# Adding the last tile's results by matmuls with a 0/1 matrix, and three moves in the order of work

## The chip, the cores and the metric

The kernel runs on one core of one Trainium2 chip. The metric is the device time of one execution in microseconds. Before the change it is 1116.69 us, the median of three runs (1115.52, 1116.69 and 1117.11).

## The reference

The input x has 4 batches of 512 rows of 256 numbers. The first half is a gated cross attention, the second a gated mixture of experts:

```python
x = x + tanh(g_xattn) * attention(layernorm(x), ctx)       # 16 heads of 64, ctx: 4 x 1024 rows,
                                                           # keys rotated by cos and sin, scores clipped to +-11
logits = xf @ wr + br                                      # xf = layernorm(x), 4 experts
gates = softmax(top_k(logits, 2))
h = gelu(xf @ w1[e] + b1[e]); y = h @ w2[e] + b2[e]        # hidden width 1024
c[e] = gelu(b1[e]) @ w2[e] + b2[e]
x = x + tanh(g_ffn) * sum_k gates_k * (y_sel - c_sel + sum_e c[e])
```

Each row of x is therefore computed by its two best experts and gets the two weighted results added.

## The kernel before, in words

Every product of two matrices of importance is done in three matmuls on numbers split into a high part (rounded to fp32r) and a low part (the remainder): high by high, high by low, low by high. The function `three` issues them. ScalarE usually makes the high part, VectorE or GpSimd the low part. There is one instruction stream for each engine, written out by hand, and semaphores join them; the order inside a stream is the order of the code.

**Start.** `before()` normalises the first context batch, turns its tiles on TensorE, and makes keys and values of the first unit. The weights for keys and values come in four parts (one for each unit of four heads) and are split by `wkv_round` (ScalarE) and `wkv_low` (VectorE, L1179). Their raw numbers share memory with the probabilities. TensorE waits once for the first part and once, at the end of `before()`, for all four.

**Attention.** Four batches, four units in each, eight steps in each unit. A step makes two score tiles (L1848), ScalarE takes their exponential (L957), VectorE clamps (L1199) and sums them (L1211, L1214), TensorE multiplies the step before by the values (L1864). In the same step TensorE makes the next unit's keys and values of one tile (`kv_make`), ScalarE brings the keys to `k_raw` (L902), GpSimd and VectorE rotate them (`rotate`, L733 and L737 on GpSimd, L1187 on VectorE), TensorE turns them (`k_turn`, L1834) and they are split (L895, L1151).

**Routing.** In the last batch, steps 17 to 26, GpSimd scatters the rows of the first three batches into slots in DRAM, sorted by expert, by indirect DMAs (`scatter`, L773): two in each of the steps 17 to 23, and in the steps 24 to 26 four, three and three. They wait for records of VectorE (`rec_out`). In the steps up to 23 a rotation follows them, in step 19 also the low part of the next query weights (`wq_low`, L722), in step 24 the low part of the output weights (`wo_low`, L726), for which SyncE's next load of output weights waits, and behind that its loads of expert weights.

**Experts.** 19 jobs (`JOBS`) of 256 slots, each with eight hidden parts m of 128 columns. For n = 8 job + m TensorE issues `outputs(n)` and then `hidden(n + 3)`. Between them ScalarE takes the Gelu (L1070), ScalarE (m in `ACT_HIGHS` = 1, 2, 3, 5, 7; L1075) or VectorE (others; L1677) makes the high part and VectorE the low part (L1680). GpSimd makes low parts of the next job's first weights (L803) and scatters the results of a finished job to the rows' places in `tokens_y` (`scatter_y`, L791), after VectorE has weighted them by the gates (`copy_slots`, L1694). The last batch's 512 rows are routed later: `rank_gates` in job 3 (m = 5), the exponential on ScalarE in job 4 (m = 6, L1105), `late_spill`, `late_bases`, `late_places` on VectorE in job 4 (m = 5, 6, 7), `last_gates`, `late_slots` with `records`, `late_owners` in job 5 (m = 5, 6, 7).

**End.** Six loads of 512 KB bring the results of the first three batches (`load_tokens`), VectorE adds them to x in the jobs 17 and 18 (`add_tokens`, L1705). After the last job its results are weighted, scattered, and then the last batch's results are loaded in eight parts of 128 KB by SyncE (L660) and ScalarE's queue (L1113), added by VectorE in eight instructions (`add_last`, L1713), and stored.

## Time and profile before

| | |
|---|---|
| median of three runs | 1116.69 us |
| profiled execution | 1115.35 us |
| its span | 1113.6 us |
| busy: PE, DVE, ACT, POOL | 1069.4, 942.0, 656.2, 530.9 us |
| granted TensorE clock, mean | 0.992 |

PE is TensorE's matmuls, DVE is VectorE, ACT is ScalarE, POOL is GpSimd, SPq and ACTq are the instructions by which SyncE and ScalarE issue DMAs. Times in the trace count from the span's start. A busy PE is one with a matmul in it; the ends of matmuls are modelled, and successive ones overlap. In square brackets stands how long the engine was idle before an instruction and what it then waited for. The granted clock is a share of 2.4 GHz, so 0.5 is the level of 1.2 GHz.

### The profile page before, as it was taken

The page shows a single profiled execution, that of the slowest core. Times are in us where ns is not written, and L with a number is a line of the kernel's source. Part 1 is how long each engine was busy: PE and PEld are TensorE (multiplying, and loading weights), DVE is VectorE, ACT ScalarE, POOL GpSimd, SP SyncE. Part 2 cuts the span into 40 slices and gives each one's busy share as a digit, 9 for nine tenths or more (in the row PEclk, how much of TensorE's full clock was granted, in tenths as well). Part 3 has the DMA queues.
Part 4 walks back from the last instruction along what each step waited for, and adds up shares of the span by engine and source line. Part 5 has one row for each costly group of instructions (what it writes and reads, how often), then busy time and mean ns, then how long its engine had stood idle before and what let it go on. Part 6 is the DMA issues. An engine that isn't in the chain of part 4 may idle for free.

```text
span 1113.6 us, 22458 instructions
## 1 busy us (share of the span) xinstructions
PE 1069.4 (96%) x7949; PEld 712.0 (64%) x7949; DVE 942.0 (85%) x1767; ACT 656.2 (59%) x1267; POOL 530.9 (48%) x550
## 2 busy tenths in 40 slices
PE   5899999999999999999999999998999998999994
PEld 3556555655555555656555655655556998899994
DVE  7798999898989989898999898888878756776675
ACT  5555556664645765554656655544667666567662
POOL 7433475332437634342565353325751654755561
PEclk9999999999999999999999999999999999999998
DMA  7000010000000000001010000601164333555335
GB/s 207 17 11 11 20 39 11 20 11 11 11 19 25 25 11 11 18 4 30 5 39 15 11 11 11 195 11 35 54 217 156 117 118 116 181 205 172 115 118 177
DMA packets 59190, 72.05 MB, mean 65 GB/s; under 512 B 11580, under 2 KB 52168, under 8 KB 59081
## 3 DMA queue, kind: packets, MB, share of 16 engines
q1 hardware_dynamic: 54840, 61.30, 17.7%
q0 software_dynamic: 3360, 8.53, 2.0%
q8 instruction: 66, 1.08, 0.4%
q10 hardware_dynamic: 880, 0.79, 0.2%
q14 instruction: 44, 0.35, 0.1%
HBM read 54.84 MB, written 16.54 MB: 64 GB/s over the span
## 4 chain that ended last, share of the span: by engine, by line
PE 80%; DVE 12%; issue 3%; ACT 2%; POOL 1%; DMA 1%; SPq 0%; DVEq 0%; ACTq 0%; POOLq 0%
PE pv L1864 17%; PE sc L1848 15%; PE kv L1793 6%; PE kv L1795 5%; PE kv L1794 5%; PE sc L1793 5%; PE sc L1794 4%; PE sc L1795 4%; PE tr L1834 3%; PE mi L1793 3%; PE mi L1794 2%; PE mi L1795 2%; DVE acc L1214 2%; PE mi L1874 2%; DVE prob L1199 1%
## 5 line engine op out<-in xcount | busy, mean ns | idle before, releaser
L957 ACT ACTIVATE prob<-sc 128x1024 f32<-128x1024 f32 x256 | 249.2, 1029 | 198.7 <-PE sc L1848 196.2
L733 POOL TENSOR_TENSOR rot_s<-k_raw,sinb 128x256 f32<-128x256 f32 x128 | 109.8, 858 | 380.8 <-ACT k_raw L902 380.5
L1864 PE MATMUL pv<-prob,val 128*32 128x512 f32 x1984 | 237.8, 597 | 0.7 <-DVE recip L1233 0.7
L1199 DVE TENSOR_SCALAR prob<-prob 128x1024 f32<-128x1024 f32 x256 | 179.7, 714 | 44.4 <-ACT prob L957 42.2
L1848 PE MATMUL sc<-q_hid,w2all 64*128 64x512 f32 x1536 | 212.5, 408 | 1.2 <-DVE w2all L1179 1.2
L1848 PEld LDWEIGHTS sc<-q_hid,w2all 64*128 64x128 f32 x1536 | 134.7, 184 | 101.2 <-issue 54.2
L1214 DVE TENSOR_TENSOR acc<-acc,prob 128x1024 f32<-128x1024 f32 x120 | 178.0, 1504 | 0.0
L737 POOL TENSOR_TENSOR rot_c<-rot_c,rot_s 128x256 f32<-128x256 f32 x128 | 111.0, 867 | 34.1 <-DVE rot_c L1187 19.1
L1864 PEld LDWEIGHTS pv<-prob,val 128*32 128x32 f32 x1984 | 54.8, 109 | 106.0 <-issue 85.6
L1793 PE MATMUL kv<-w2all,acts 128*128 128x512 f32 x248 | 109.7, 442 | 2.2 <-DVE acts L1145 1.3
L1795 PE MATMUL kv<-w2all,acts 128*128 128x512 f32 x248 | 98.7, 398 | 0.0
L1794 PE MATMUL kv<-w2all,acts 128*128 128x512 f32 x248 | 98.0, 395 | 0.0
L1793 PE MATMUL sc<-w2all,q_hid 128*128 x304 | 89.9, 296 | 7.5 <-DVE q_hid L1680 6.0
L1794 PE MATMUL sc<-w2all,q_hid 128*128 x304 | 86.1, 283 | 0.0
L1795 PE MATMUL sc<-w2all,q_hid 128*128 x304 | 85.8, 282 | 0.0
L1211 DVE TENSOR_TENSOR acc<-prob 128x1024 f32<-128x1024 f32 x60 | 84.5, 1447 | 0.0
L902 ACT ACTIVATE k_raw<-kv 128x256 f32<-128x256 f32 x124 | 48.6, 392 | 53.5 <-PE kv L1795 51.6
L1187 DVE TENSOR_TENSOR rot_c<-kv,cosb 128x256 f32<-128x256 f32 x124 | 52.3, 422 | 31.6 <-ACT val L903 25.8
L1680 DVE SCALAR_TENSOR_TENSOR q_hid<-sc,rot_c,q_hid 128x256 fp32r<-128x256 f32 x78 | 37.5, 482 | 35.7 <-ACT q_hid L1075 30.3
L1793 PEld LDWEIGHTS sc<-w2all,q_hid 128*128 128x128 f32 x304 | 58.0, 191 | 11.5 <-issue 11.2
L1070 ACT ACTIVATE sc<-sc,c_aff 128x256 f32<-128x256 f32 x78 | 34.9, 448 | 51.4 <-PE sc L1795 51.4
L803 POOL TENSOR_TENSOR acts<-prob,acts 128x512 fp32r<-128x512 f32 x34 | 44.8, 1319 | 40.5 <-ACT acts L990 39.4
(326 smaller groups left out, 2400.0 us busy)
## 6 DMA issues: line engine op xcount, KB each, us to landing
prob<-in_L_ffn_w SPq DMA_DIRECT2D x17, 1024.0 KB
slots_x<-lat_r SPq DMA_DIRECT2D x1, 5016.0 KB, 18.9
rows<-slots_x SPq DMA_DIRECT2D x19, 264.0 KB, 5.2
rows<-in_ctx SPq DMA_DIRECT2D x32, 128.0 KB, 2.2
w_raw<-in_L_xattn_Wq SPq DMA_DIRECT2D x16, 256.0 KB, 2.7
w_raw<-in_L_xattn_Wo SPq DMA_DIRECT2D x64, 64.0 KB
acc<-in_L_ffn_w SPq DMA_DIRECT2D x16, 256.0 KB, 5.0
acc<-in_L_ffn_w SPq DMA_DIRECT2D x5, 512.0 KB
```

What stands on the lines that cost most here:

```text
L733: g.tensor_tensor(rot_s[:].rearrange("p (h a c) -> p h a c", h=4, a=2), kh[:, :, ::-1, :], sinb[:, t].unsqueeze(1).to_broadcast([P, 4, 2, ...
L737: g.tensor_tensor(k_rot[:], rot_c[:], rot_s[:], ALU.add).then_inc(rot, 1)
L957: a.activation(prob[:, s % 2, i, :], sc[i][:], ACT.Exp, scale=DH ** -0.5).then_inc(exp_done[i], 1)
L1187: v.tensor_tensor(rot_c[:].rearrange("p (h c) -> p h c", h=8), kv_bank(b, u, t)[:, 0:UW].rearrange("p (h c) -> p h c", h=8), cosb[:, t].un ...
L1199: v.tensor_scalar(prob[:, s % 2, i, :], prob[:, s % 2, i, :], EXP_LOW, EXP_HIGH, ALU.max, ALU.min).then_inc(clamped[i], 1)
L1211: v.tensor_tensor(acc[:, i, :], prob[:, 0, i, :], prob[:, 1, i, :], ALU.add).then_inc(summed[i], 1)
L1214: v.tensor_tensor(acc[:, i, :], acc[:, i, :], prob[:, s % 2, i, :], ALU.add).then_inc(summed[i], 1)
L1793: mm(dst, lhs(0), rhs(0), start=start, stop=False, **kw)
L1794: mm(dst, lhs(0), rhs(1), start=False, stop=False, **kw)
L1795: return mm(dst, lhs(1), rhs(0), start=False, stop=stop, **kw)
L1848: last = mm(sc[i][:, h * N:(h + 1) * N], kst[rows_h, u % 2, j, lk, t * P:(t + 1) * P], q_sp[rows_h, p % 2, lq, :], start=lk + lq == 0, sto ...
L1864: last = mm(out_bank(b, p)[g * 32:(g + 1) * 32, :], val[:, u % 2, 2 * c + i, at:at + 32], prob[:, s % 2, i, h * N:(h + 1) * N], start=c == ...
```

## The change

1. **The last tile.** The results of the last job (`LAST`) aren't scattered any more. All their rows belong to the last batch. ScalarE and VectorE weight them by the gates and split them in high and low, VectorE has built a matrix that is 1 where a slot's row is (`one_hot`, from `last_places` and an iota of GpSimd, in job 18 at m = 3), and 16 matmuls with it as the stationary operand add up the rows in two banks, from which `add_last` adds them to x. The other tiles' results for the last batch are loaded in two DMAs of 512 KB, once job 17 is scattered, into the memory of the raw weights, and added by `add_rows`. Places of `tokens_y` that nobody writes any more must be zero, so SyncE clears those of the last batch in the last batch's step 8 (1 MB). In job 18 ScalarE makes all high parts, `copy_slots` of job 17 comes at m = 1 instead of 2, and `add_tokens` at m = 0, 2, 4, 6 instead of 1, 3, 5, 7. The second half of job 18's output goes to another bank.
2. **Late gates.** The exponential of the last batch's logits is computed by GpSimd as a power of e, in its stream ahead of the scatter of job 2's results. `last_gates` moves to job 3 (m = 7), `late_places` to job 4 (m = 6), `late_slots`, `records` and `late_owners` in job 5 one m earlier.
3. **First weights.** TensorE waits for the part of unit u when it makes its first tile, the last `wkv_low` moves to the end of `before()`, the first exponentials wait for the parts whose raw numbers they overwrite, and ScalarE copies the affine vectors ahead of the first `wkv_round`.
4. **Scatters.** In the last batch a step's scatters come after its rotation.

```diff
+        z_rows = pall[:, 0:2 * 4 * D].rearrange("p (r i d) -> p r i d", r=2, d=D)
+        slot_no = pall[:, 4 * N:5 * N]
+        hot = q_hid[:, 4 * N:6 * N].rearrange("p (i n) -> p i n", i=2)
+        y_sp = q_hid[:, 6 * N:8 * N].rearrange("p (i l d) -> p i l d", i=2, l=2)
+        local = r_keep[:, 28:32].rearrange("p (a i) -> p a i", a=2)
...
+        def highs_of(job):
+
+            return tuple(range(MT)) if job == LAST else ACT_HIGHS
+
+        def out_of(job, i):
+
+            if job == LAST and i:
+                return mi[:, 0:D]
+            return yb[job % 2][:, i * D:(i + 1) * D]
...
+                    for r in range(2):
+                        at = r * TOKENS + (B - 1) * N
+                        sp.dma_start(ys_d[at:at + N, :].rearrange("(t p) d -> p t d", p=P),
+                                     blank[:, 0:D].unsqueeze(1).to_broadcast([P, NT, D])).then_inc(slots_clear, 16)
...
-            def load_last(i):
-
-                if i == 0:
-                    sp.wait_ge(y_done[0], 32 * ((JOBS + 1) // 2))
-                    sp.wait_ge(y_done[1], 32 * (JOBS // 2))
-                at = (B - 1) * N + i * P
-                sp.dma_start(rows[:, i, 0:D], ys_d[at:at + P, :]).then_inc(ld_z[i], 16)
+            def load_last():
+
+                sp.wait_ge(y_done[0], 32 * (JOBS // 2))
+                sp.wait_ge(y_done[1], 32 * (JOBS // 2))
+                sp.wait_ge(w_low, JOBS - 1)
+                for r in range(2):
+                    at = r * TOKENS + (B - 1) * N
+                    sp.dma_start(z_rows[:, r], ys_d[at:at + N, :].rearrange("(i p) d -> p i d", p=P)).then_inc(ld_z, 16)
...
             for b in range(B - 1):
+                if b == B - 2:
+                    load_last()
...
             for i in range(0, NT, 2):
-                sp.wait_ge(z_took, 2 * i + 2)
...
-                    pool.wait_ge(slots_clear, 16)
+                    pool.wait_ge(slots_clear, 48)
...
+            def late_exps():
+
+                base = mhalf[:, 4:5]
+                g.memset(base, math.e).then_inc(f_eps, 1)
+                pool.wait_ge(f_eps, 3)
+                pool.wait_ge(f_diff, 2)
+                g.tensor_tensor(f_tmp[:, EARLY:, :], base.unsqueeze(2).to_broadcast([P, NT, E]), f_logit[:, EARLY:, :],
+                                ALU.pow).then_inc(f_exp, 1)
+
             def scatter_y(k):

                 pool.wait_ge(y_copied, k + 1)
+                if k == 0:
+                    pool.wait_ge(slots_clear, 48)
...
-                if last:
-                    for n in range(*SCATTERS_AT.get(i, (0, 0))):
-                        scatter(n)
                 if u == 0 and s == STEPS - 1 and not is_first(b, u):
                     loop_scale(b)
                 if make:
                     rotate(*next_unit(b, u), s)
+                if last:
+                    for n in range(*SCATTERS_AT.get(i, (0, 0))):
+                        scatter(n)
...
+                if job == LATE_RANK + 1:
+                    late_exps()
                 if job > 1:
                     scatter_y(job - 2)
+            g.iota(slot_no, pattern=[[1, N]], base=0, channel_multiplier=0,
+                   allow_small_or_imprecise_dtypes=True).then_inc(const2, 1)
             scatter_y(JOBS - 2)
-            scatter_y(JOBS - 1)
...
+                if is_first(b, u) and s < 2:
+                    act.wait_ge(wkv_ready, 2 * s + 2)
...
                     act.dma_start(affine_raw[i * KT:(i + 1) * KT, :], v.rearrange("(k p) -> k p", p=P)).then_inc(ld_aff, 16)
-                wkv_round(0)
                 act.wait_ge(aff_turned, 1)
                 a.activation(affine[:].rearrange("p v k -> p (v k)"), mi[:, 0:4 * KT], ACT.Copy).then_inc(aff_ready, 1)
+                wkv_round(0)
                 act.wait_ge(aff_ready, 1)
...
-                if m in ACT_HIGHS:
+                if m in highs_of(job):
...
-                if job == LATE_RANK + 1 and m == 6:
-                    act.wait_ge(f_diff, 2)
-                    a.activation(f_tmp[:, EARLY:, :], f_logit[:, EARLY:, :], ACT.Exp).then_inc(f_exp, 1)
...
-            act.wait_ge(y_done[0], 32 * ((JOBS + 1) // 2))
-            act.wait_ge(y_done[1], 32 * (JOBS // 2))
-            act.wait_ge(y_took, 2 * (B - 1))
-            for i in range(NT):
-                at = TOKENS + (B - 1) * N + i * P
-                act.dma_start(more[:, i, 0:D], ys_d[at:at + P, :]).then_inc(ld_z[i], 16)
+            act.wait_ge(y_mm, JOBS * MT)
+            for i in range(2):
+                a.activation(y_sp[:, i, 0], out_of(LAST, i), ACT.Copy,
+                             scale=sel[:, LAST % 4, i, 0:1]).then_inc(y_high, 1)
             for i in range(1, NT, 2):
-                act.wait_ge(z_took, 2 * i + 2)
+                act.wait_ge(z_took, 2 + i // 2 + 1)
...
-                    if t in (2, 6, 8, 10):
-                        wkv_low((2, 6, 8, 10).index(t))
+                    if t in (2, 6, 8):
+                        wkv_low((2, 6, 8).index(t))
...
+                wkv_low(UNITS - 1)
...
-            def add_last(i):
-
-                dve.wait_ge(ld_z[i], 16 * 2)
-                row = xacc[:, EARLY + i, :]
-                for r in range(2):
-                    wait(dve, z_took, 2 * i + r)
-                    v.tensor_tensor(row, row, (rows, more)[r][:, i, 0:D], ALU.add).then_inc(z_took, 1)
+            def last_places():
+
+                chain(v.tensor_scalar(local[:, 0], sel[:, LAST % 4, :, 1], float(FAR - (B - 1) * N), None, ALU.add))
+                chain(v.tensor_scalar(local[:, 1], local[:, 0], float(TOKENS), -float(TOKENS), ALU.is_ge, ALU.mult))
+                chain(v.tensor_tensor(local[:, 0], local[:, 0], local[:, 1], ALU.add))
+
+            def one_hot(i):
+
+                if i == 0:
+                    dve.wait_ge(const2, 7)
+                    dve.wait_ge(h_mm, LAST * MT)
+                v.tensor_scalar(hot[:, i], slot_no, local[:, 0, i:i + 1], None, ALU.is_equal).then_inc(hot_ready, 1)
+
+            def split_last(i):
+
+                dve.wait_ge(y_high, i + 1)
+                v.scalar_tensor_tensor(y_sp[:, i, 1], out_of(LAST, i), sel[:, LAST % 4, i, 0:1],
+                                       y_sp[:, i, 0].bitcast(F32), ALU.mult, ALU.subtract).then_inc(y_copied, 1)
+
+            def add_rows(r):
+
+                dve.wait_ge(ld_z, 32)
+                wait(dve, z_took, r)
+                dst = xacc[:, EARLY:, :]
+                v.tensor_tensor(dst, dst, z_rows[:, r], ALU.add).then_inc(z_took, 1)
+
+            def add_last(half):
+
+                dve.wait_ge(cs_mm, half + 2)
+                dve.wait_ge(z_took, 2)
+                dst = xacc[:, EARLY + 2 * half:EARLY + 2 * half + 2, :].rearrange("p t d -> p (t d)")
+                v.tensor_tensor(dst, dst, hb[half][:], ALU.add).then_inc(z_took, 1)
...
-                if m == 2 and job:
+                if job and m == (1 if job == LAST else 2):
...
                     choose(job + 1)
+                    if job + 1 == LAST:
+                        last_places()
...
+                    if m == 7:
+                        last_gates(EARLY, B * NT)
...
                         late_bases()
-                    if m == 7:
                         late_places()
...
                     if m == 5:
-                        last_gates(EARLY, B * NT)
-                    if m == 6:
                         late_slots()
                         records(EARLY)
-                    if m == 7:
+                    if m == 6:
                         late_owners()
...
-                if job == 17 and m in (5, 7):
+                if job == LAST - 1 and m in (5, 7):
                     add_tokens(m // 7)
-                if job == 18 and m % 2:
+                if job == LAST and m % 2 == 0:
                     add_tokens(2 + m // 2)
-            copy_slots(JOBS - 1)
-            for i in range(NT):
-                add_last(i)
+                if job == LAST and m == 3:
+                    one_hot(0)
+                    one_hot(1)
+            dve.wait_ge(y_mm, JOBS * MT)
+            for i in range(2):
+                split_last(i)
+            for r in range(2):
+                add_rows(r)
+            for half in range(2):
+                add_last(half)
...
+                if b == 0 and t == 0:
+                    pe.wait_ge(wkv_ready, u + 1)
...
-                        pe.wait_ge(wkv_ready, 1)
...
-                pe.wait_ge(wkv_ready, UNITS)
...
-                    last = three(yb[job % 2][:, i * D:(i + 1) * D], lambda l: hid_sp[:, n % 4, l, i * P:(i + 1) * P],
-                                 lambda l: w2_of(expert[0], m, l), m == 0 and i == 0, m == MT - 1 and i == 1,
+                    last = three(out_of(job, i), lambda l: hid_sp[:, n % 4, l, i * P:(i + 1) * P],
+                                 lambda l: w2_of(expert[0], m, l), m == 0 and (i == 0 or job == LAST), m == MT - 1 and (i == 1 or job == LAST),
...
+            pe.wait_ge(hot_ready, 2)
+            for half in range(2):
+                for i in range(2):
+                    for l in range(2):
+                        if half == l == 0:
+                            pe.wait_ge(y_high, i + 1)
+                        if half == 0 and l == 1:
+                            pe.wait_ge(y_copied, JOBS - 1 + i + 1)
+                        for t in range(2):
+                            at = (2 * half + t) * P
+                            last = mm(hb[half][:, t * D:(t + 1) * D], hot[:, i, at:at + P], y_sp[:, i, l, :],
+                                      start=i == l == t == 0, stop=i == l == t == 1, skip_group_check=True)
+                last.then_inc(cs_mm, 1)
```

## Rows read from the trace of the kernel before

**Rows 1.** Page, part 1: engine, busy us (share of the span), instructions

```profile
PE 1069.4 (96%) x7949; PEld 712.0 (64%) x7949; DVE 942.0 (85%) x1767; ACT 656.2 (59%) x1267; POOL 530.9 (48%) x550
```

**Rows 2.** Timeline of the start: start, length, engine, line, operation, [idle before]

```profile
36.45 2.32 DVE L1179 TENSOR_TENSOR w2all<-prob,w2all 128x512 fp32r<-128x512 f32 x2
...
38.83 1.67 PE L1848 MATMUL sc<-q_hid,w2all 64*128 64x512 f32 x12 [1.24 <-DVE w2all L1179]
```

**Rows 3.** Timeline, last batch, around the first scatters

```profile
763.63 0.38 ACT L902 ACTIVATE k_raw<-kv 128x256 f32<-128x256 f32 x1 [1.04 <-PE kv L1795]
...
765.43 1.39 POOL L773 DMA_INDIRECT slots_x<-more,route  x1 [2.47 <-DVE rows L1489]
...
766.23 0.42 DVE L1187 TENSOR_TENSOR rot_c<-kv,cosb 128x256 f32<-128x256 f32 x1
...
767.13 1.84 POOL L773 DMA_INDIRECT slots_x<-more,route  x1 [0.30 <-issue]
...
771.01 0.44 PE L1834 MATMUL tr<-ident,rot_c 128*128 128x128 f32 x2 [2.33 <-POOL rot_c L737]
```

**Rows 4.** Windows: PE, PEld, DVE, ACT, POOL busy, PEclk, DMA share, GB/s

```profile
772.00:775.50 3.50, 3.50 (x15) 3.21 (x14) 1.50 (x4) 0.94 (x3) 2.89 (x4) 0.51 0.21 77
```

**Rows 5.** Timeline, last batch, steps behind the scatters

```profile
791.85 0.44 PE L1834 MATMUL tr<-ident,rot_c 128*128 128x128 f32 x2
...
814.92 1.30 POOL L726 TENSOR_TENSOR wo<-w_raw,wo 128x512 fp32r<-128x512 f32 x1
...
820.27 0.39 PE L1793 MATMUL mi<-wo,acts 128*128 128x256 f32 x1
```

**Rows 6.** Timeline, jobs 4 and 5, around the late exponential

```profile
917.98 1.28 ACT L1105 ACT_TABLE_LOAD   x1
...
919.51 1.28 ACT L1070 ACT_TABLE_LOAD   x1
...
922.49 1.19 DVE L1594 TENSOR_SCALAR lat_r<-lat_r 128x16 f32<-128x16 f32 x1
...
922.51 0.38 PE L1793 MATMUL sc<-w2all,q_hid 128*128 x1 [0.67 <-DVE q_hid L1680]
...
926.00 0.38 PE L1793 MATMUL sc<-w2all,q_hid 128*128 x1 [1.80 <-DVE q_hid L1680]
```

**Rows 7.** Groups by line and form, GpSimd: shapes, count, busy, mean ns, idle

```profile
L717 POOL TENSOR_TENSOR l_rs<-l_rs,mhalf 128x4 f32<-128x4 f32 x4 | 4.0, 1011 | 0.3
...
L752 POOL TENSOR_TENSOR f_stats<-f_stats,mhalf 128x8 f32<-128x8 f32 x1 | 2.9, 2853 | 0.1
```

**Rows 8.** Timeline: a power of one column, and job 3's end

```profile
10.68 0.55 POOL L698 TENSOR_TENSOR c_rs<-c_rs,mhalf 128x1 f32<-128x1 f32 x1
...
905.63 0.17 DVE L1468 TENSOR_TENSOR f_gates<-f_gates 128x16 f32<-128x16 f32 x1
...
911.13 0.28 PE L1793 MATMUL sc<-w2all,q_hid 128*128 x1
```

**Rows 9.** Timeline of the end

```profile
1097.84 0.48 DVE L1680 SCALAR_TENSOR_TENSOR q_hid<-pv,rot_c,q_hid 128x256 fp32r<-128x256 f32 x1 [0.35 <-ACT q_hid L1075]
...
1098.24 1.22 DVE L1705 TENSOR_TENSOR xacc<-xacc,more 128x1024 f32<-128x1024 f32 x1
...
1099.16 0.28 PE L1795 MATMUL sc<-w2all,q_hid 128*128 x1
...
1099.48 0.88 DVE L1694 TENSOR_SCALAR acc<-sc,sel 128x256 f32<-128x256 f32 x2
...
1104.49 1.76 SPq L660 DMA_DIRECT2D rows<-tokens_y  x4
...
1111.05 0.42 DVE L1713 TENSOR_TENSOR xacc<-xacc,more 128x256 f32<-128x256 f32 x1
```

**Rows 10.** Timeline: an addition of 512 columns from PSUM

```profile
861.34 0.75 DVE L1244 SCALAR_TENSOR_TENSOR xacc<-mi,gates,xacc 128x512 f32<-128x512 f32 x1 [0.44 <-PE mi L1795]
```

**Rows 11.** Tile tokens_y, 1072 to 1082 us: its loads of 512 KB

```profile
DMA to landing us min/median/max: 3.9/4.9/5.9
```

16 lines of the change are left out of this document (10 added, 6 removed).

## The prediction

> **What bounds the kernel now.** I read the shares on the page of the profile first: TensorE is busy 1069.4 of 1113.6 us [rows 1], the next engine 85% of it. So a change pays only where TensorE stands, and before and after its work. I then listed every stretch in which no matmul runs. They add up to about 44 us, and three places and the end hold what this change touches. In the start, TensorE waits 1.24 us before the first scores [rows 2]. In the last batch, it waits 2.33 us for a rotated key tile [rows 3], and the granted clock is then 0.51 (the 1.2 GHz level) for 3.5 us [rows 4]. In the expert part, two waits of 0.67 and 1.80 us follow two table loads on ScalarE [rows 6]. The tail is the big one: the last matmul starts at 1099.16 and ends at 1099.44, the span ends at 1113.6, so 14.2 us are a serial chain of copy, scatter, load, add and store [rows 9].
>
> **Start.** The change lets TensorE wait for the split of key and value weights unit by unit, and moves the last split behind the rotation and the key split. Now the last split (two instructions, 2.32 us) holds the first scores to 38.83 although the keys and queries are there [rows 2]. Afterwards the scores start 1.24 earlier. The second pair of exponentials gets the new wait, for the fourth split; exponentials behind it on ScalarE belong to the second step, some 3 us later than the first, while the split ends at about 40.8, so the wait is hidden. But clamping the first probabilities now stands behind the moved split on VectorE and gains nothing, and the next rotation comes from there. So between 0.5 and 1.24; I take 1.0. Reading the affine vectors before the first rounding gains nothing: the DMA of the weights ends that wait in either order.
>
> **Scatters behind rotation.** In the last batch GpSimd now issues two scatters (1.39 and 1.84 us) before it rotates the tile whose raw keys lie ready at 764.01 [rows 3]. Rotated first, the tile is done when VectorE's cosine product (ends 766.65) and one GpSimd addition are, at about 767.5, and TensorE wants it at 768.69: the 2.33 go. With them goes, I think, the slow stretch. In it 3.5 us at clock 0.51 did what takes some 1.9 at full clock, so 1.6 more [rows 4]. Next late is VectorE, which was idle for only some 2 us after the gap, and has tenths to spare later; so I count 3.5 of the 3.9, with 2.3 as the low end if the clock falls elsewhere.
> *What the move delays.* Each of the seven scatter pairs comes one rotation later, and the last pair falls behind the last rotation: it adds its 1.8 + 1.8 us in front of ten further scatters and of the low part of the output weights, now at 814.92. That becomes 818.5 to 819.8, and the projection needs it at 820.27 [rows 5]: covered by 0.5 us. SyncE's next weight loads wait for the same instruction and start 3.6 later; ScalarE rounds the first of them at 824.09, I expect it landed at 825.5, and the next exponentials start at 826.67, so 1 us of cover. Within a step, rotation (1.7), scatters (3.6) and where it applies a 2.3 us weight split must fit: in the fourth rotated step they push the next rotation by 0.5, and it had 1.5 to spare before 791.85.
> The rule that speaks against this is that of the Trainium skill, SBUF — State Buffer, section "SBUF: two separate sides": a GpSimd DMA's descriptors can't be written while VectorE holds the shared port pair. The rows agree that a scatter is stretched (1.84 beside VectorE's work against 0.97 alone). By that rule moved scatters could all be the long kind; the third rival prices it without the rule.
>
> **Late gates.** The exponential of the last four row tiles leaves ScalarE. Two table loads and a small activation occupied ScalarE from 917.98 to 920.79, 2.8 us, and TensorE then waited 0.67 and 1.80 us [rows 6]. Without them the Gelu there runs 1.8 us earlier, but VectorE takes its place: the placing of late rows (five small instructions, one stretched to 1.19 beside GpSimd) now stands in the slot before, so the next low part comes only 0.3 earlier and the first wait shrinks to about 0.4. The second wait goes, since nothing stands ahead of the next job's first split. I take 2.0, low end 1.0, high end 2.5. (By the Trainium skill, ScalarE: Activation LUTs, "What ACT_TABLE_LOAD costs", a switch has a drain of 1380 ns beside its 1283, 5.3 us for two. The rows show the activation directly behind the load, so 2.8 stands; by the Trainium skill up to 2.5 more would leave ScalarE, and TensorE's wait caps what that can give, so the gain here would be 2.5 instead of 2.0.)
> *Price of the power.* GpSimd raises e to 16 columns. One column took 0.55 alone [rows 8], four 1.01, eight 2.85 with a blocked stretch in it [rows 7]: 0.15 a column gives 2.9 us, proportion from the eight-column row 5.7, from four 4.0. I take 2.9, since the one and four column rows are undisturbed. It starts when the differences are there, 905.80, and ends at 908.8. VectorE's normalising of the gates, moved two jobs ahead, waits for that, and behind it stand the two splits of the next hidden tile: 908.8 + 1.0 + 1.0 = 910.8. TensorE wants that tile at 911.13 [rows 8]. So up to 3.2 us the power is free; above, each us costs one. Queued behind it on GpSimd are one result scatter and a weight split with 4 us to spare.
>
> **Tail.** Before: copy 0.88, two indirect scatters, landing, eight loads, eight adds, stores. Now the last tile is split high (ScalarE) and low (VectorE), a 0/1 matrix sends it through 16 matmuls to its rows, and the other tiles' rows were loaded early.
> Last job: VectorE drops three high parts (0.48 each) but its adds of 1.22 us stand one slot earlier. The last add sits directly in front of the last low part, at 1097.84 now; 1097.1 + 1.22 = 1098.35, so that low part, and the last matmul, slip 0.5, to 1099.9. Then two high copies (0.4 each, from PSUM, pipelined), two low ones at 0.45: to 1101.3. Two adds over all four row tiles, 1.22 each [rows 9]: 1103.8. The 16 matmuls, 0.12 apart (0.24 if the clock is low), end by 1103.7 at worst: covered. Two adds from PSUM at 0.75 [rows 10]: 1105.3. From the last add's end to the span's end it is 1113.60 − 1111.47 = 2.1: 1107.4.
> The early load can be last instead. Job 17's copy ends at about 1091.1; scatters and landing took 4.1 from a copy's end to the next load (1100.36 to 1104.49), so the two 512 KB loads start at 1095.3. Such loads landed in 3.9 to 5.9 us, the latter when queued behind another [rows 11], and a store of 512 KB is in flight: 1100.5 to 1101.5, against 1101.3. I add 0.2: span part ends at 1107.6, 6.0 less. Bounds 4.5 and 7.0.
> Clearing 1 MB of the results' buffer lies 60 us ahead of its first reader: nothing. Building the two rows of the 0/1 matrix and the places falls into VectorE's idle time: nothing.
>
> **The sum.** 1.0 + 3.5 + 2.0 + 6.0 = 12.5 us. The profiled execution took 1115.35 (span 1113.6 and 1.75 around it), 1.3 below the median of 1116.69; by its own time it is 1102.9. The gain is the same for the median: 1116.69 − 12.5 = 1104.2.
>
> **Rivals.**
> 1. The forecast: 1104.2, own range 1102 to 1106. Chance 0.54.
> 2. The early load binds: stores and loads share the DMA engines, whose share was 0.9 to 1.0 while such transfers overlapped. Lands 1.5 to 2 later: 1105.9. For it: it is due within 0.2 us of need. Chance 0.13.
> 3. The moved scatters carry the wait on: late weight split, projection and late key rotation give back 2.5. 1106.7. For it: only 0.5 us of cover; against: every other step has over 1. Chance 0.14.
> 4. The power is dear: at the eight-column rate 5.7 us, 2.5 over the cover: 1106.7. Chance 0.09.
> 5. Slower than before: the power with a base that isn't −0.5's fixed exponent runs a longer path. From 3.2 + 12.5 = 15.7 us on (about 1 us a column) everything is eaten; a wait so long is followed by the clock's slow stretch (1.6). At 1.1 a column, 17.6 us: 1104.2 + 14.4 + 1.6 = 1120.2. For it: nothing but that no row has this base; against: 0.15 a column. Chance 0.03.
> 6. It doesn't do what it says: the waits at rotation or tables have another cause and stay, 5.5 of the sum missing: 1109.7. Chance 0.04.
> 7. All bounds good: 1101.9. Chance 0.03.
>
> **How the numbers follow.** The likeliest gives 1104.2. From 1101.5 to 1107.9 the range holds cases 1, 2, 7 and most of 3 and 4. About 0.2% (2 us) is what a measurement of this kernel can tell from no change. Slower is case 5 and a little for mishaps that I don't see, 0.04; same 0.02; the rest faster.
>
> **What the profile would show.** Right: first scores at about 37.6; no wait above 0.5 us for rotation in the last batch and clock 1.00 there; two table loads instead of four, the power under 3.2 us; last matmul of the last job to the end of the span under 8.5 us, VectorE's adds back to back. Wrong: a wait of VectorE on the load of the rows (rival 2), a projection that waits for output weights (3), VectorE idle ahead of the gates (4, 5).

## The result, and the profile after

The change makes the kernel faster, by less than forecast. Its median is 1109.77 us (1109.58 to 1111.31) against 1116.9 for the kernel before, ratio 0.9938, 95% interval [0.9925, 0.9952]: 7.1 us, where the prediction had 12.5 and no less than 8.8. The profiled execution took 1109.79, span 1108.1.

The page of the changed kernel, span and busy time of each engine [rows 1]:

```profile
span 1108.1 us, 22494 instructions
PE 1069.2 (96%) x7965; PEld 712.2 (64%) x7965; DVE 946.6 (85%) x1765; ACT 655.8 (59%) x1269; POOL 532.3 (48%) x551
```

TensorE is as busy as before, so all of the difference is in its waits and in the end. I lined up the two traces by the same work (raw keys of each tile copied out, Gelu of each hidden tile) and read at each how much earlier the new kernel stands; below this is called "by events". In the start it gains 1.5 us (0.2 of it ahead of the changed place); in the scatter stage 1.2; in the expert jobs up to the last 1.0; behind that 1.9. Together that is 5.6, the difference of the spans (1113.62 and 1108.06). Between the start and the last job each of the two traces has one stretch at half clock, so the clock makes no difference between them there. (The medians differ by 7.1, since before's profiled execution was 1.5 below its median.)

Timeline of the start [rows 2]. The wait of 1.24 is gone and the first scores begin 1.48 earlier:

```profile
36.98 0.44 PE L1906 MATMUL tr<-ident,rot_c 128*128 128x128 f32 x2 [0.38 <-POOL rot_c L761]
37.35 1.66 PE L1920 MATMUL sc<-q_hid,w2all 64*128 64x512 f32 x12
```

Timeline of the scatter stage [rows 3]. A number in brackets is the wait ahead of the row and what ended it. The 2.33 is gone, the scatter starts behind the rotation, and three waits have grown or are new, the largest ahead of the tile whose rotation (L757) starts only when the sixth pair of scatters is out:

```profile
765.62 1.93 PE L1936 MATMUL pv<-prob,val 128*32 128x512 f32 x16 [0.63 <-DVE recip L1268]
768.11 2.00 POOL L797 DMA_INDIRECT slots_x<-more,route  x1 [0.20 <-issue]
771.38 0.38 PE L1863 MATMUL mi<-wo,acts 128*128 128x256 f32 x1 [0.49 <-DVE q_hid L1229]
...
801.16 1.81 POOL L797 DMA_INDIRECT slots_x<-rows,route  x1
803.27 1.48 POOL L797 DMA_INDIRECT slots_x<-rows,route  x1 [0.30 <-issue]
804.77 0.76 POOL L757 TENSOR_TENSOR rot_s<-k_raw,sinb 128x256 f32<-128x256 f32 x1
807.26 0.44 PE L1906 MATMUL tr<-ident,rot_c 128*128 128x128 f32 x2 [0.92 <-POOL rot_c L761]
```

Table by stretches (busy time of each engine, then granted clock, DMA share, GB/s). The slow stretch of [rows 4] isn't there any more. Another one is, 35 us ahead of it, in the midst of dense matmuls:

```profile
734.00:736.00 2.00, 2.00 (x16) 1.76 (x17) 0.49 (x1) 0.00 (x0) 0.00 (x0) 0.86 0.00 0
736.00:738.00 2.00, 2.00 (x9) 1.25 (x8) 0.69 (x1) 1.74 (x2) 0.00 (x0) 0.50 0.00 0
738.00:740.00 2.00, 2.00 (x8) 1.57 (x8) 0.69 (x1) 0.50 (x2) 0.00 (x0) 0.78 0.02 4
```

Timeline of the expert jobs [rows 6, 8]. The power takes 2.93 us. TensorE's waits between 900 and 970 us are 0.40, 1.18, 1.38, 0.27 and 2.04, together 5.3, as much as before (5.4). Ahead of the third, ScalarE stands still for 3.42 us although its input is ready at 935.0, and nothing in the trace releases it. At the last, four small VectorE instructions run from 947.98 to 949.63, beside a weight split of GpSimd:

```profile
903.30 2.93 POOL L817 TENSOR_TENSOR f_gates<-mhalf,f_gates 128x16 f32<-128x16 f32 x1 [3.36 <-DVE f_gates L1504]
921.03 0.38 PE L1863 MATMUL sc<-w2all,q_hid 128*128 x1 [1.18 <-DVE q_hid L1717]
938.28 0.45 ACT L1110 ACTIVATE sc<-sc,c_aff 128x256 f32<-128x256 f32 x1 [3.42 <-remote]
939.99 0.38 PE L1863 MATMUL sc<-w2all,q_hid 128*128 x1 [1.38 <-DVE q_hid L1717]
947.96 1.37 POOL L838 TENSOR_TENSOR acts<-prob,acts 128x512 fp32r<-128x512 f32 x1
947.98 1.65 DVE L1589 SCALAR_TENSOR_TENSOR lat_r<-r_keep,b1t 128x48 f32<-128x48 f32 x4
951.85 0.38 PE L1863 MATMUL sc<-w2all,q_hid 128*128 x1 [2.04 <-DVE q_hid L1717]
```

Timeline of the end [rows 9]. Job 17's scatters are out at 1090.54, but their landing lets SyncE go on only at 1094.6; the z rows are there at 1100.8, VectorE waits 3.70 us for them with both splits done, and behind the last add (1104.75) come 3.35 us, where before showed 2.1:

```profile
1087.43 1.83 POOL L826 DMA_INDIRECT tokens_y<-acc,target  x1 [6.50 <-DVE acc L1731]
1089.57 0.97 POOL L826 DMA_INDIRECT tokens_y<-acc,target  x1 [0.30 <-issue]
1094.64 0.92 SPq L684 DMA_DIRECT2D prob<-tokens_y  x2
1095.35 0.28 PE L1865 MATMUL mi<-w2all,q_hid 128*128 x1
1096.64 0.47 DVE L1760 SCALAR_TENSOR_TENSOR q_hid<-mi,sel,q_hid 128x256 fp32r<-128x256 f32 x1
1100.81 2.55 DVE L1768 TENSOR_TENSOR xacc<-xacc,prob 128x1024 f32<-128x1024 f32 x2 [3.70 <-DMA prob<-tokens_y]
1104.07 0.68 DVE L1775 TENSOR_TENSOR xacc<-xacc,sc 128x512 f32<-128x512 f32 x1
```

### The profile page after: what moved, and what is told of

Same layout as the page of the kernel before. It is cut to its first block, busy times and chain, and to the rows that moved or that the text cites. A ratio compares the mean times of both kernels' runs of the same rounds, so it can differ in the third digit from the quotient of the medians.

```text
span 1108.1 us, 22494 instructions
## 1 busy us (share of the span) xinstructions
PE 1069.2 (96%) x7965; PEld 712.2 (64%) x7965; DVE 946.6 (85%) x1765; ACT 655.8 (59%) x1269; POOL 532.3 (48%) x551
## 4 chain that ended last, share of the span: by engine, by line
PE 78%; DVE 14%; issue 3%; ACT 2%; DMA 1%; POOL 1%; another core or an unknown queue 0%; SPq 0%; DVEq 0%; POOLq 0%
PE pv L1936 16%; PE sc L1920 15%; PE kv L1863 6%; PE kv L1865 5%; PE kv L1864 5%; PE sc L1863 4%; PE sc L1865 4%; PE sc L1864 4%; PE tr L1906 3%; DVE acc L1249 3%; PE mi L1863 3%; PE mi L1864 2%; PE mi L1865 2%; PE mi L1946 2%; DVE prob L1234 2%
## 5 line engine op out<-in xcount | busy, mean ns | idle before, releaser
L757 POOL TENSOR_TENSOR rot_s<-k_raw,sinb 128x256 f32<-128x256 f32 x128 | 110.4, 862 | 380.7 <-ACT k_raw L940 380.6
L1234 DVE TENSOR_SCALAR prob<-prob 128x1024 f32<-128x1024 f32 x256 | 183.2, 729 | 40.5 <-ACT prob L997 38.1
L1863 PE MATMUL sc<-w2all,q_hid 128*128 x296 | 87.2, 295 | 7.3 <-DVE q_hid L1717 6.5
L1864 PE MATMUL sc<-w2all,q_hid 128*128 x296 | 83.8, 283 | 0.0
L1865 PE MATMUL sc<-w2all,q_hid 128*128 x296 | 83.6, 282 | 0.0
```

Of the source, the lines that this page charges most:

```text
L757: g.tensor_tensor(rot_s[:].rearrange("p (h a c) -> p h a c", h=4, a=2), kh[:, :, ::-1, :], sinb[:, t].unsqueeze(1).to_broadcast([P, 4, 2, ...
L1234: v.tensor_scalar(prob[:, s % 2, i, :], prob[:, s % 2, i, :], EXP_LOW, EXP_HIGH, ALU.max, ALU.min).then_inc(clamped[i], 1)
L1863: mm(dst, lhs(0), rhs(0), start=start, stop=False, **kw)
L1864: mm(dst, lhs(0), rhs(1), start=False, stop=False, **kw)
L1865: return mm(dst, lhs(1), rhs(0), start=False, stop=stop, **kw)
```

## The experiments

They were measured in five groups, each beside the kernel before, and each group on another chip (0, 3, 13, 1 and 9; for the first measurement the record names none). Only kernels of one group are compared by their times, across groups by their ratios. "Waits" is the sum of TensorE's waits of over 0.15 us between 900 and 970 us; "end" is the time from the first 0/1 matmul to the span's end. Both are of the one profiled execution. Where the text compares two variants of the change and says nothing else, their intervals overlap, and the traces carry the reading.

| group, before | kernel | median us | ratio [95%] | waits | end |
|---|---|---|---|---|---|
| 1, 1115.41 | e1 change | 1106.39 | 0.9925 [0.9911, 0.9938] | 2.5 | 12.2 |
| | e2 stores behind | 1104.51 | 0.9908 [0.9893, 0.9923] | 2.5 | 9.8 |
| | e3 without tail | 1108.58 | 0.9938 [0.9924, 0.9952] | 2.5 | |
| | e4 one pair behind | 1105.28 | 0.9909 [0.9894, 0.9924] | 2.5 | 11.7 |
| 2, 1114.04 | e5 stores after landing | 1105.01 | 0.9926 [0.9911, 0.9941] | 2.4 | 10.1 |
| | e6 halves | 1104.95 | 0.9927 [0.9913, 0.9942] | 2.5 | 10.1 |
| | e7 without gates | 1108.34 | 0.9952 [0.9935, 0.9969] | 5.3 | 11.5 |
| | e8 before | 1114.60 | | 5.3 | |
| 3, 1116.44 | e9 without scatter | 1113.09 | 0.9980 [0.9969, 0.9991] | 5.4 | 11.3 |
| | e10 new end | 1110.08 | 0.9947 [0.9928, 0.9965] | 6.1 | 9.0 |
| | e11 tokens earlier | 1112.32 | 0.9965 [0.9953, 0.9977] | 5.5 | 9.1 |
| | e12 change | 1111.68 | 0.9956 [0.9940, 0.9973] | 5.4 | 12.1 |
| 4, 1117.02 | e13 late scatters later | 1123.73 | 1.0056 [1.0039, 1.0073] | 7.0 | 12.0 |
| | e14 change | 1111.58 | 0.9953 [0.9937, 0.9970] | 4.5 | 11.8 |
| | e15 new end | 1108.89 | 0.9927 [0.9911, 0.9944] | 4.5 | 9.0 |
| | e16 without gates | 1110.04 | 0.9948 [0.9931, 0.9965] | 5.6 | 11.9 |
| 5, 1116.19 | e17 start alone | 1113.65 | 0.9978 [0.9969, 0.9987] | 5.3 | |
| | e18 new end, no gates | 1109.40 | 0.9937 [0.9922, 0.9951] | 5.4 | 9.1 |

### What is in the kernel, and what is chance: e1, e12, e14, e8

> The changed kernel once more, unchanged. Its first trace shows two losses that no part of the change explains: a stretch at half clock at 734.8 to 739 us inside dense work (some 1.6 us), and a ScalarE gap of 3.42 us at 934.85 that nothing in the trace released (with it a TensorE wait of 1.38 us in job 4). Theory: both fall by chance, so this trace has them at other places or not at all, and span differs by up to 1.6 us. Rival: they belong to the kernel; then both stand at the same places within 1 us. Time 1109.8 (1108 to 1111.5) either way.

e1 took 1106.39, 3.4 below the first measurement, with a before that was 1.5 lower too. Its granted clock is 1.00 from 734 to 740 (the slow stretch is at 20 to 24 instead), and ScalarE has no gap. In the place of three waits (1.38, 0.27, 2.04) stands one:

```profile
934.09 0.45 ACT L1110 ACTIVATE sc<-sc,c_aff 128x256 f32<-128x256 f32 x1 [0.22 <-PE sc L1865]
944.55 0.56 DVE L1589 SCALAR_TENSOR_TENSOR lat_r<-r_keep,b1t 128x48 f32<-128x48 f32 x4
947.35 0.38 PE L1863 MATMUL sc<-w2all,q_hid 128*128 x1 [0.84 <-DVE q_hid L1717]
```

The same Gelu runs 4.2 earlier than in the first trace, where e1 was ahead by 1.0 until then, and the four small VectorE instructions take 0.56, since they fall between two instructions of GpSimd and not beside one. So both of the losses that I couldn't assign are not fixed parts of the kernel.

> The changed kernel a third time, unchanged. The six runs of the first measurement (1109.6 to 1111.3) stand 3.3 us above the five of e1 (1105.6 to 1107.5), as the ScalarE gap of 3.42 us in the first trace would make them. Theory (the gap depends on how the program came to lie in memory when it was loaded, and then holds for all its runs): these runs fall all together at one of the two levels, and the trace has the gap at 935 us if it is the upper one. Rival (a chance of each run): a mix of both levels within these runs.

> The changed kernel, unchanged, as the base of this group. Theory (a level of the whole measurement): either 1106.4 and no ScalarE gap near 935 us, or 1109.5 to 1112 and the gap of 3.4 us there, with e13, e15 and e16 on the same side. Rival (chance of each run): mixed.

e12's six runs are 1110.41 to 1112.09 and e14's four 1110.86 to 1112.55: all high, as the first theory has it. e12's trace has the gap (3.41 at 938.66). e14's has a shorter one further on, and the four instructions collide with GpSimd's weight split and take 2.31 together, and TensorE's longest wait follows:

```profile
944.29 0.45 ACT L1110 ACTIVATE pv<-pv,c_aff 128x256 f32<-128x256 f32 x1 [1.58 <-issue]
947.07 2.31 DVE L1589 SCALAR_TENSOR_TENSOR lat_r<-r_keep,b1t 128x48 f32<-128x48 f32 x4
951.59 0.58 PE L1863 MATMUL sc<-w2all,q_hid 128*128 x1 [2.56 <-DVE q_hid L1717]
```

So there are two levels, and a whole group is on one: every kernel with the late gates has waits of 2.5 us in groups 1 and 2, and 4.5 to 7.0 in groups 3 and 4 and in the first measurement. What sets the level isn't known. Since every group is a chip of its own, and none was measured twice, chip and measurement can't be told apart; that the program's place in memory sets it fits less well, since different kernels of a group agree. The kernel before moves too: its medians are 1115.41 and 1114.04 in groups 1 and 2, and 1116.19 to 1117.02 in the others.

> The kernel before, unchanged, for its trace alone: where does it run at half clock. The first trace had stretches at 20.5 to 24.5 and 772 to 775.5 us, and the changed kernel in five traces one at 20 to 30, one at 734 to 740, or both. Theory (the stretch at 772 follows the 2.33 us wait on the scatters): it stands there again within 1 us, and none at 734 to 740. Rival (a stretch falls once or twice a run by chance, in 20 to 30 and in 730 to 780, whatever the kernel): it stands at 734 to 740 here, or is missing.

```profile
738.00:740.00 2.00, 2.00 (x14) 1.46 (x14) 0.00 (x0) 0.73 (x1) 0.00 (x0) 0.73 0.00 0
740.00:742.00 2.00, 2.00 (x9) 1.37 (x6) 1.09 (x2) 1.31 (x2) 0.00 (x0) 0.50 0.00 0
...
772.00:774.00 2.00, 0.08 (x2) 0.00 (x0) 2.00 (x3) 1.64 (x2) 1.86 (x3) 1.00 0.18 68
774.00:776.00 2.00, 1.60 (x8) 1.38 (x9) 1.56 (x3) 0.00 (x0) 1.69 (x2) 1.00 0.00 0
```

The rival holds: the kernel before, with its wait of 2.32 us at 772 (TensorE busy 0.08 of 2 us), runs at the full clock behind it, and is at half clock from 738.9 to 742.3, where the changed kernel usually is. Over all 20 traces a stretch at the 1.2 GHz level begins between 18 and 30 us in 17, between 734 and 740 in 16, and behind the wait at 772 in one of the four that have that wait. One costs 1.5: from 732 to 754 us e1, at full clock, takes 21.83, e2 with the stretch 23.37. This doesn't show that the wait has no part in it. The three traces that have the wait and no stretch behind it (e8, e9, e17) had one that ended about 30 us ahead of it (at 742.3, 739.4 and 741.4), and the trace with the stretch behind the wait had none there. Whether one keeps the next away wasn't tested. What counts for the change is how many there are: each of the four traces with the wait has one between 734 and 776 us, of the 16 without it 13 have one. By these counts taking the wait away saves about a fifth of a stretch, 0.3 us.

### The end: e3, e2, e5, e6, e11

> The start, the scatters behind rotation and the late gates of the change, with the old end (job 18's copy, its scatters, the eight loads and adds). It prices the tail part by its absence. Theory from the events of the two traces: the tail part is worth 2.0 us only, since the wait for the z rows took the rest: 1111.8 us (1111 to 1112.8). Rival (the tail is worth the 6.0 us of the prediction and the loss lies elsewhere): 1115.8.

```diff
-            for i in range(2):
-                split_last(i)
-            for r in range(2):
-                add_rows(r)
-            for half in range(2):
-                add_last(half)
+            copy_slots(JOBS - 1)
+            for i in range(NT):
+                add_last(i)
```

(All of the tail part, on each engine, goes back to the old code.) 2.2 slower than e1: the tail part is worth about 2.2 and not 6.0, as its theory had it (2.0). The intervals of e1 and e3 overlap a little (0.9924 to 0.9938), but a gain of 6.0 is far outside.

> Only the order on SyncE's queue at the end is changed: the two loads of the last tile's rows (z rows) are issued ahead of the three stores of finished batches, not between the second and third. Theory (the stores fill the DMA engines while job 17's scattered rows land, 4.1 us behind the last scatter where before showed 1.1, and delay the z rows by that): loads issued at 1091.7 in place of 1094.6, landed by 1096.5 to 1097.4, VectorE's wait of 3.70 us ahead of the adds gone, span end 3 to 3.7 us earlier: 1106.3 us (1105.6 to 1107.2). Rival (the scatter's landing takes 4 us of itself, or the loads do): the loads go out at 1094 still and the time stays 1109.8 within 0.7. Second rival: the held stores now collide with the last four stores and give half of the gain back: 1108.

```diff
+            load_last()
             for b in range(B - 1):
-                if b == B - 2:
-                    load_last()
                 sp.wait_ge(y_took, 2 * b + 2)
```

1.9 faster than e1, half of what was expected. Timeline of its end:

```profile
1086.20 0.97 POOL L825 DMA_INDIRECT tokens_y<-acc,target  x1 [0.30 <-issue]
1088.79 0.91 SPq L684 DMA_DIRECT2D prob<-tokens_y  x2
1095.49 2.55 DVE L1767 TENSOR_TENSOR xacc<-xacc,prob 128x1024 f32<-128x1024 f32 x2 [1.75 <-DMA prob<-tokens_y]
```

From the end of the second scatter (1087.17) to the loads it is 1.6 us, where e1 has 4.4 (1086.00 to 1090.36) and the first trace 4.1. So the late landing was the stores' doing, as the theory says: two stores of 512 KB stood ahead, issued by 1088.8 in the first trace, so SyncE then waited 5.9 us for the end of the scatters (1090.54) and their landing. The loads' own time didn't shrink: 6.7 from issue to the first add, against 6.3 in e1.

> As e2, and SyncE also waits until the z rows have landed before it issues the three stores of the finished batches, so that no store shares the DMA engines with the z loads. In e2 the loads went out 1.6 us sooner than in e1 but landed 6.7 us later (6.3 in e1), leaving 1.75 us of VectorE's wait. Theory (the stores slow the loads themselves too): landing 4.5 us after issue, about 1093.3, no wait of VectorE left, last add ends 1.7 us sooner than in e2: 1102.8 us (1102.2 to 1104). Rival (1 MB from the scattered rows takes over 6 us of itself): the same as e2, 1104.5. Second rival: 1.5 MB of stores now stand beside the last stores and lengthen the end by more than 1.7: 1105 or more.

```diff
             load_last()
+            sp.wait_ge(ld_z, 32)
             for b in range(B - 1):
```

```profile
1088.39 0.91 SPq L684 DMA_DIRECT2D prob<-tokens_y  x2
1094.59 2.55 DVE L1768 TENSOR_TENSOR xacc<-xacc,prob 128x1024 f32<-128x1024 f32 x2 [0.93 <-DMA prob<-tokens_y]
1097.85 0.68 DVE L1775 TENSOR_TENSOR xacc<-xacc,sc 128x512 f32<-128x512 f32 x1
```

The theory falls: with no store beside them the z loads still take 6.2 us. Two loads of 512 KB cost that much of themselves here, and the stores of e2 add 0.5 at most. And the second rival is there: from the last add's end (1098.53) to the span's end (1102.9) it is 4.4, against 3.3 in e2, since 1.5 MB of stores are now in the way. Its end, 10.1, is no better than e2's 9.8.

> As e5, and the adds go by halves: the two z adds and the PSUM add of row tiles 0 and 1, then those of 2 and 3 (six adds of 512 columns instead of two of 1024 and two of 512), so that the stores of tiles 0 and 1 leave earlier. The time from the last add to the end was 2.14 us in e3 (stores one by one) and 3.3 in e1 (four within a microsecond). Theory (the four stores share the DMA engines): the tail behind the last add shrinks by 0.8 to 1.2, the two more adds cost 0.3: 0.7 us faster than e5. Rival: the store's time is fixed at this size and the kernel is 0.3 slower than e5.

```diff
-            for r in range(2):
-                add_rows(r)
             for half in range(2):
-                add_last(half)
+                for r in range(2):
+                    add_rows(half, r)
+                add_last(half)
```

1104.95 beside 1105.01, and both ends are 10.1: counted from the first 0/1 matmul the last add ends 0.7 later (6.4 against 5.7), and what comes behind it is 0.7 shorter (3.6 against 4.4 us). Neither theory nor rival by its size.

> As e10, but the six adds of the finished batches go in job 17 m = 1, 3, 5, 7 and job 18 m = 0, 2 (before: job 17 m = 5, 7, job 18 m = 0, 2, 4, 6), so that their loads and stores run some 6 us sooner, with SyncE's queue in the order of the change (two stores ahead of the z loads). Theory (the late scatter landing and the slow end are shares of the same DMA engines, busy over 0.9 from 1084 to 1088): scatter lands within 2 us, the stores are over before the z loads: z rows land at 1093, 1.3 us sooner than e10, and the last stores run alone: 1101.3 us (1100.5 to 1102.5). Rival (VectorE cannot take two more adds in job 17 without making the lows late): waits of TensorE of over 1 us in job 17 and 1103 or more.

```diff
-                if job == LAST - 1 and m in (5, 7):
-                    add_tokens(m // 7)
-                if job == LAST and m % 2 == 0:
-                    add_tokens(2 + m // 2)
+                if job == LAST - 1 and m % 2:
+                    add_tokens(m // 2)
+                if job == LAST and m in (0, 2):
+                    add_tokens(4 + m // 2)
```

(On top of e10, with the change's own queue order.) 2.2 slower than e10, and the one trace of each differs by 1.7. The landing is as expected: scatter's end 1095.14, loads at 1096.47, 1.3 us with the stores ahead of them but long over. The end, 9.1, gains nothing, since there VectorE's adds are the chain. The rival is right in kind: TensorE waits 0.51, 0.25 and 0.35 for low parts between 1083 and 1087, where e10 has no wait. That is 1.1 us and not the whole loss; e11's trace also has 3.4 us more at half clock than e10's (6.8 from 734.5 beside 3.4 from 952.0), so the rest can be the clock's.

### The scatters: e9, e4

> The change without its scatter part: scatters issued ahead of rotation in every step, as before. Theory from the events of e8 and e1: the part removes the wait of 2.32 us at 772 and brings 0.45 (values, 764), 0.49 (projection, 770) and 0.92 (a later tile, 805), so that 743 to 854 us shows no gain: the same as the change within 0.5 us, beside e1's 1106.4. The prediction's own size was 3.5, of which 1.6 was the half-clock stretch: 1109.9. Middle case (the wait alone counts, 1.9): 1108.3.

```diff
+                if last:
+                    for n in range(*SCATTERS_AT.get(i, (0, 0))):
+                        scatter(n)
                 if make:
                     rotate(*next_unit(b, u), s)
-                if last:
-                    for n in range(*SCATTERS_AT.get(i, (0, 0))):
-                        scatter(n)
```

1.4 slower than e12 in its group (2.7 by the ratios, 0.9980 and 0.9956, whose intervals still overlap, from 0.9969 to 0.9973). By events it is 1.2 between 740 and 863 us. In the pair e8 and e1 the same stage gives nothing (4.53 and 4.48 us ahead), in the first two traces 1.2. So the part brings 0 to 1.2 by the traces, neither the 3.5 of the prediction nor a plain nothing.

> Scatters issued behind rotation only in the first step that scatters (where the 2.33 us wait of before stood); in the later steps they are ahead of rotation again, as before. Theory: the new TensorE wait of 0.92 us at 806.34 comes from the pair of scatters at 801.16 to 804.75 that now stands ahead of the next tile's rotation; with the old order there it goes and the first step's gain stays: 0.9 us faster than the change, 1108.9 us. Rival: with the old order in the later steps the 2.33 us wait comes up one step later (the scatters catch up): 1111 or more. Third: 1109.8 within 0.4, the wait hidden by later ones.

```diff
+                first = last and i == SCATTER + 1
+                if last and not first:
+                    for n in range(*SCATTERS_AT.get(i, (0, 0))):
+                        scatter(n)
                 if make:
                     rotate(*next_unit(b, u), s)
-                if last:
+                if first:
                     for n in range(*SCATTERS_AT.get(i, (0, 0))):
                         scatter(n)
```

```profile
777.33 0.44 PE L1910 MATMUL tr<-ident,rot_c 128*128 128x128 f32 x2 [0.43 <-POOL rot_c L761]
```

1.1 faster than e1. The wait of 0.92 is gone and one of 0.43 has come at 777: with its own slow stretch taken off, e4 stands 0.7 us better at 863. The mechanism holds: scatters behind one rotation stand ahead of the next. In e10 and e15 the same order shows another 0.45 at 806 and so gains less.

### The late gates: e7, e16, e13, e18

> The change without its late-gates part: the exponentials on ScalarE in job 4 between two GELU loads, the gates in job 5 as before. Theory from the events: TensorE's waits between 900 and 970 us sum to 5.4 in before and to 2.5 in e1, so the part is worth 2.9: 1109.3 us (1108.8 to 1110) beside e1's 1106.4. The prediction's own size was 2.0: 1108.4. Rival (the GELU loads are hidden by the queue of matmuls): under 1 us, 1107.

```diff
-                if job == LATE_RANK + 1:
-                    late_exps()
...
+                if job == LATE_RANK + 1 and m == 6:
+                    act.wait_ge(f_diff, 2)
+                    a.activation(f_tmp[:, EARLY:, :], f_logit[:, EARLY:, :], ACT.Exp).then_inc(f_exp, 1)
```

Ratio 0.9952 beside e1's 0.9925: 3.0 us, and the waits are 5.3 against 2.5. From the Gelu of the 21st hidden tile to that of the 81st (about 883 to 985 us) e7 takes 100.0 us and each of e1 to e6 97.3. On this level the part is worth 2.7 to 2.9, more than the 2.0 predicted.

> The kernel of e7 (no late-gates part) beside e14. Theory A (the gap belongs to the late-gates part's instructions): where e14 has the gap, this has none at that instruction, and is no slower than e14 (within 0.7): the part is worth 3.0 less 3.3. Theory B (the gap is of the chip and the stage, not of the part): the gap stands here too within two jobs, and this is 2 to 3 us slower than e14, as e7 was than e1 (1.95 by the medians).

On the other level no gain can be seen: 1110.04 without it, 1111.58 with it, and the intervals are nearly the same. Neither theory is right as put. ScalarE's gap at that place is absent from e16 (theory A), and its waits, 5.6, sum to those of e7. But e16 is slower than e7 all the same: between the same two Gelus it takes 101.8 us against 100.0, and before takes 101.8 against e8's 99.95, both by 1.8. The sum of the waits hides this, since they lie elsewhere. e16 has these two, which e7 and e8 don't have; before, e17 and e18 have the first as well (0.40, 0.40, 0.41):

```profile
941.96 0.38 PE L1855 MATMUL sc<-w2all,q_hid 128*128 x1 [0.41 <-DVE q_hid L1708]
961.93 0.38 PE L1855 MATMUL sc<-w2all,q_hid 128*128 x1 [0.71 <-DVE q_hid L1708]
```

So the upper level is in every kernel, and costs 1.8 us without the late gates. With them it costs 3.5 (the first trace, 100.8 against e1's 97.3), and 5.1 and 5.5 in e12 and e14 (102.4 and 102.8), which also have a stretch at half clock there. The part is then worth from +1.0 to -1.0. It shifts VectorE's and ScalarE's work there against GpSimd's: in the 6 traces without the part the four VectorE instructions take 0.56, in 4 of the 14 with it 1.65 to 2.3, and ScalarE's gap of 3.4 stands in 5 of those 14 (the first trace, e9 to e12) and in none of the 6.

> The change with the eight scatters of the last tile's rows put one job later (behind the weight splits of jobs 7, 8 and 9, not of 6, 7 and 8), so that no scatter runs on GpSimd or the DMA engines between 930 and 938 us beside the 1 MB weight load but the two of job 4's results. Theory (the ScalarE gap comes from DMA traffic that delays something it waits for, such as its own instructions): where e14 has the gap at 935, this has none, and is 3 us faster. Rival (it belongs to the place in the program): the gap stands unchanged and the time is e14's within 0.5. Where e14 has no gap: the same time.

```diff
-        LATE_SCATTERS = {6: (0, 3), 7: (3, 6), 8: (6, 8)}
+        LATE_SCATTERS = {7: (0, 3), 8: (3, 6), 9: (6, 8)}
```

```profile
977.60 1.09 PE L1989 MATMUL tr<-ident,rows 128*128 128x128 f32 x4 [9.88 <-DMA rows<-slots_x]
```

12.2 slower than e14 (the intervals are far apart), and for a reason I had not in view: the slots' rows of a coming job are read from what these scatters write, with no job to spare, and TensorE waits 9.88 us for them. ScalarE's gap is absent here, but VectorE's collision is there (1.66) and the waits are 7.0, so this run doesn't tell whether traffic makes the gap.

> e4's order of scatters and e2's order of SyncE, and at the end: the two z loads have a semaphore each, VectorE adds the PSUM of half 0 first, then the z rows of rank 0 as soon as they land, the PSUM of half 1, and the z rows of rank 1 by halves with the stores behind each. Theory (what bounds the end is the scatter's landing and 1 MB of z rows, 6.2 to 6.7 us from issue, then the adds behind it, then 3.3 us of stores): VectorE's last add ends 1.5 to 2 us sooner than in e2, and e4's order is worth 0.6: 1102.3 us (1101.5 to 1103.2). Rival (the DMA engines are full with the 1.5 MB of stores until 1098.5 whatever the adds do): 0.6 to 1.0 faster than e2 only, 1103.7.

> The kernel of e10 again, beside e14. e10's end ran 9.0 us from its first 0/1 matmul to the end of the span, against 12.1 in e12 and 9.8 in e2, and e4's order of scatters was worth 0.6 in trace: 3.1 + 0.6 = 3.7 us faster than e14 if both show in the same measurement. Rival: e10 was only 1.6 faster than e12 by the medians, and stays so, the rest lost between 950 and 970 us.

```diff
-            for r in range(2):
-                add_rows(r)
-            for half in range(2):
-                add_last(half)
+            add_last(0, 0)
+            add_rows(1, 0, 0, NT)
+            add_last(2, 1)
+            add_rows(3, 1, 0, 2)
+            add_rows(4, 1, 2, 4)
```

(With e2's queue order, e4's scatters, and a semaphore for each z load.) The times missed the figures, since group 3 was on the high level, but the end did what was meant: 9.0 us in both, against 12.1 and 11.8. e10 is 1.6 faster than e12, e15 2.7 faster than e14 (the intervals of either pair still overlap). Timeline of e15's end; the wait for the z rows is gone and VectorE goes from add to add:

```profile
1099.89 0.69 DVE L1778 TENSOR_TENSOR xacc<-xacc,kv 128x512 f32<-128x512 f32 x1 [0.68 <-PE kv L2209]
1100.68 1.23 DVE L1771 TENSOR_TENSOR xacc<-xacc,prob 128x1024 f32<-128x1024 f32 x1
1102.01 0.69 DVE L1778 TENSOR_TENSOR xacc<-xacc,sc 128x512 f32<-128x512 f32 x1
1102.81 1.49 DVE L1771 TENSOR_TENSOR xacc<-xacc,prob 128x512 f32<-128x512 f32 x2
```

In both groups this kernel is clearly faster than the kernel before, and its median is below the change's.

> The kernel of e10 and e15 without the late-gates part (the exponentials on ScalarE, the gates in job 5, as before). By the lower level (as in e1 to e7): e7 1108.3 less 3.1 (end) and 0.6 (scatters), 1104.6, ratio 0.992. By the upper level (as e14 to e16): e16 1110.0 less 2.7 (e15 beside e14), 1107.3, ratio 0.9915. Theory: the ratio is 0.991 to 0.992 on either, where e10 and e15 with the gates had 0.9947 and 0.9927. Rival (the gaps of ScalarE come back at other places with this layout too): 0.994 or more.

Ratio 0.9937 [0.9922, 0.9951]: within a hair of the rival's 0.994, not in the theory's 0.991 to 0.992. The end is 9.1 and the waits 5.4, as they should be. Its group has no changed kernel beside it, but e17 and e18 have the wait of 0.40 and 0.41 us near 946 that marks the upper level in before and e16, and 1116.19 for the kernel before fits that level. e10 and e15, on the same level with the gates, had 0.9947 and 0.9927: leaving the late gates out is no clear gain either.

### The start: e17

> The kernel before with only the start's part (weights awaited one by one). Theory from event times (the k of every tile stands 1.5 us earlier from 42 us on, in all traces of the change): 1.5 us faster than before in the same measurement, ratio 0.9987, and TensorE's wait of 1.24 us at 37.6 is gone. The prediction's size: 1.0. Rival (later stages, tied to something else, take it back): no difference.

```diff
+                    if b == 0 and t == 0:
+                        pe.wait_ge(wkv_ready, u + 1)
...
-                pe.wait_ge(wkv_ready, UNITS)
```

(ScalarE's waits, its order and the place of the last split go with it, as in the change.) Ratio 0.9978 [0.9969, 0.9987]: 2.5 us, and the interval just holds the 1.5 expected. The first raw keys behind the first scores are copied out at 41.16, beside 42.30 and 44.08 in the two traces of before; with what stood at 35 us already taken off, 1.3 and 2.8. e8 has a further slow stretch at 39 to 43, directly behind the 1.24 us wait that this part removes; by one trace of two that may be the rest.

## Why the prediction was wrong

By events the first measurement has 1.3, 1.2, 1.0 and 1.9 us where the sum had 1.0, 3.5, 2.0 and 6.0. The tail is the step that failed most: the forecast issued the early load in time, and it came late.

**Start: 1.0, measured 1.3.** The mechanism is right and the term a little too small (2.5 by e17's times). The clamp of the first probabilities does stand behind the moved split, but it starts at 39.77, 1.13 ahead of before's 40.90: I had it gain nothing.

**Scatters: 3.5, measured 0 to 1.2.** Two steps failed. The 1.6 for the slow stretch rested on one trace: that a stretch followed the wait was taken for a cause. Its price was right (1.5), but it isn't bound to the wait: e8, e9 and e17 have the wait and no stretch behind it, and 13 of the 16 traces without the wait have a stretch at 734 to 740 instead, the first measurement's among them. The forecast had named this as its low end (2.3, if the clock falls elsewhere). And of the 2.33 most came back as 0.92, 0.43 more on the values and 0.49 on the projection. I had named that mechanism (rival 3) and looked for it at the wrong place: the low part of the output weights, on whose 0.5 us of cover I dwelt, came at 816.00 to 817.3, with 1.4 to spare, while "every other step has over 1" was the sentence that failed. In the step ahead of 806 the pair took 3.6 us, and the rotation behind it came late.

**Late gates: 2.0, measured 2.9 in groups 1 and 2, 1.0 or nothing elsewhere.** The power's 2.93 us is as predicted, it was done at 906.23, and the two table loads are gone. In groups 1 and 2 the gain is 2.9, above the high end. In the first measurement 3.5 us are lost against e1 between 935 and 957 us, in groups 3 and 4 up to 5.5, to a gap of ScalarE, to a collision of VectorE with GpSimd and, in groups 3 and 4, to the clock; kernels without the part lose 1.8 between 935 and 967, so 1.7 to 3.7 of it fall on the part. That rival wasn't in the list. It is the largest piece that separates the first measurement from e1.

**Tail: 6.0, measured 2.2 (e3), by events 1.5 to 1.9.** This is the step with the largest error, 4 us. The splits, adds and matmuls took what the rows of before said; the last low part slipped 0.40 (0.5 predicted). Wrong was the place of the early load. I took 4.1 us from the copy to the loads, as before showed; the first scatter took 1.83 (0.9 more than alone) and the landing 4.1 instead of 1.1. So the loads were issued 1.0 us ahead of the end of TensorE's last matmul of job 18 (1094.64 and 1095.63) and not 4.6. Rival 2 was this one, with its sign right ("stores and loads share the DMA engines") and less than half its size (1.7, where VectorE waited 3.7): I let the stores slow the loads, and e5 shows that they do so by 0.5 at most; they hold up the scatter's landing ahead of them. The Trainium skill, DMA: Bandwidth & Descriptors, section "Latency and other measured facts", says that a transfer's fixed cost is mostly the round trip to the memory that it writes, and that this grows when that memory is loaded, from 0.2 to 2 us. The traces agree in kind: 1.1 us in before and 1.3 to 1.6 with the stores out of the way (e2, e5, e11), 4.0 to 4.6 with them, more than the page's figure; whether it is the loaded memory or the queue ahead, no run tells. The last stores cost the rest: four at once take 3.3 where one by one took 2.1.

**The range.** It ended at 8.8 below before; the first measurement gave 7.1, e1 gave 9.0 and e12 and e14 4.8 and 5.4. The rivals were taken one at a time, and the likelier of them give back 1.7 to 2.5 each. What happened was several losses together: the early load, the late rotations, the clock elsewhere, and in the expert jobs one that wasn't in the list. They had been given no chance in company, though they lean on the same thing, cover of about 1 us read from a single trace. That rival 6 named 1109.7, the time measured first, is luck: by it the waits at rotation and tables stay, and both are gone.

**What stays open.** What sets the level of a group, and what ScalarE waits for in the gap of 3.4 us, which no semaphore in the trace ends. A fetch of instructions was looked for: no such packet moves between 930 and 940 us in the first trace. The level may be the chip's, since every group ran on one of its own; the same two kernels on two chips, twice each, would tell. Whether DMA traffic is behind it wasn't settled (e13). Why the half-clock stretch falls at 734 to 740, behind 0.5 us of wait at 731.8 and in dense work, isn't known either. By the Trainium skill, TensorE: Matmul & The Clock Gate, section "HAM oscillation — how this bites in real kernels", the lower clock comes back where matmuls in short bursts wait for a DMA; e13 agrees, whose wait of 9.88 us for a DMA has the lower clock in it and behind it. The other traces differ, since here it comes in dense work in 16 of 20, and doesn't behind a wait of 2.3 us in three of four, though those three had a stretch some 30 us earlier.

## What to carry to other kernels

When a chain at the end is cut short by an early load, follow that load back to the last write that it must await, and ask what else is in the DMA queues then: moving two stores behind it gave back 1.9 us, and taking the PSUM adds into the wait shortened the end from 9.8 to 9.0. A gain read from one trace is worth its cover only: where engines meet within 1 us, a shift of a stage by 3 us can make a new collision as easily as it removes an old one, and several such rivals come true together. A slow stretch of the clock that stands once behind a wait need not go when the wait goes; look at a second execution first. And sums of waits can be alike where the waits aren't: line the traces up by the same work.

## What the runs showed of the hardware

- The landing of an indirect scatter of 128 rows, from the end of its issue to the waiting queue's next instruction: 1.1 to 1.6 us with no store ahead or the stores long over, 4.0 to 4.6 with 1 MB of stores ahead.
- Two loads of 512 KB issued together are usable 6.2 to 6.7 us after the issue of the first, with stores beside them or without.
- Four small VectorE instructions (128x48) take 0.56 us alone and 1.65 to 2.3 beside an elementwise instruction of GpSimd; it is the second of the four that is held up, 1.3 to 1.95 us in place of 0.2.
- Raising a number to a power on GpSimd with e as the base and 16 columns: 2.93 us, 0.16 for each column beyond the four of the 1.01 us power, against 0.15 a column between the one and four column powers with an exponent of -0.5.
- A wait of TensorE of 9.88 us (e13, to 977.6) has the 1.2 GHz level from 972.0 to 982.2; waits of 2.0 to 2.6 near 951 are followed by 3.4 to 6.2 us of it in five of eight traces, those of 1.8 near 926 in one of six.
